# Second graph-attention layer: 2048 of its destinations through a dense edge matrix, edge weights kept in one place

## What is computed

```
h = x @ W                                   # 6250 x 64
logits = leaky_relu(al_s[src] + al_d[dst], 0.2)
alpha = exp(logits - max) / sum(exp(logits - max))     # per destination, self-loops included
out = segment_sum(h[src] * alpha, dst) + b
x = layernorm(x + (out @ Wf + bf))
```

## Time and profile before

| | us |
|---|---|
| median of 3 runs | 7316.36 |
| lowest, highest | 7312.23, 7317.64 |
| profiled execution, its span (no other time is given for it) | 7334.6 |
| PE, DVE, ACT, POOL busy in it | 6062.9, 3365.6, 1425.8, 5086.1 |

### The profile page before, as it was taken

The page is one execution under the profiler, slowest core; times in us unless marked ns, Lnnn a source line. Parts: engine busy times, 40 slices in busy tenths (PEclk is TensorE's granted clock), DMA queues, the critical chain, the costliest instruction groups (busy, mean ns, idle before and its releaser), DMA issues. The chain is left out here.

```text
span 7334.6 us, 120792 instructions
## 1 busy us (share of the span) xinstructions
PE 6062.9 (83%) x30188; PEld 4280.8 (58%) x30188; DVE 3365.6 (46%) x13118; ACT 1425.8 (19%) x5109; POOL 5086.1 (69%) x4839
## 2 busy tenths in 40 slices
PE   3888888886728888867877779998899999988997
PEld 2555555555615555556666656665566656665665
DVE  4444444443436666645555544444233323333444
ACT  2333333332201222212222211111000100010001
POOL 3777777777737777757777757665777677767776
PEclk9887888887869999965555569998999999999998
DMA  8988899884324444433333359885999799979996
GB/s 290 217 186 187 183 191 188 185 184 109 93 83 114 117 116 116 116 77 81 82 81 80 83 159 303 284 282 177 308 311 308 240 316 307 303 240 318 312 318 216
DMA packets 767060, 1440.91 MB, mean 196 GB/s; under 512 B 157272, under 2 KB 484876, under 8 KB 764212
## 3 DMA queue, kind: packets, MB, share of 16 engines
q1 hardware_dynamic: 474532, 886.97, 35.9%
q0 software_dynamic: 289936, 523.75, 32.0%
q10 hardware_dynamic: 2304, 26.74, 0.9%
HBM read 1140.97 MB, written 295.98 MB: 196 GB/s over the span
## 5 line engine op out<-in xcount | busy, mean ns | idle before, releaser
L736 POOL DMA_INDIRECT rows<-gcn_rows,index x1632 | 1550.7, 950 | 664.1 <-issue 457.4
L1277 POOL DMA_INDIRECT rows<-gat_rows,index x1568 | 1500.6, 957 | 646.1 <-issue 459.4
L832 PEld LDWEIGHTS bank<-onehots,rows 128*128 128x128 f32 x8704 | 1146.5, 194 | 598.0 <-issue 539.2
L1608 POOL DMA_INDIRECT support<-rows,index x784 | 1218.7, 1554 | 388.0 <-DMA support<-rows,index 188.2
L832 PE MATMUL bank<-onehots,rows 128*128 128x128 f32 x8704 | 1185.4, 279 | 150.0 <-DVE onehots L881 66.5
L1408 PE MATMUL bank<-onehots,rows 128*128 128x128 f32 (+1 forms) x4704 | 949.6, 339 | 325.3 <-DVE rows L1484 325.1
L1408 PEld LDWEIGHTS bank<-onehots,rows 128*128 128x128 f32 (+1 forms) x4704 | 722.7, 203 | 527.2 <-issue 322.2
L844 PE MATMUL dense_bank<-matrix,edge_space 128*128 128x512 f32 x1792 | 891.2, 619 | 0.0
L1747 PE MATMUL rows_bank<-x_window,cross 128*128 128x256 f32 x1568 | 649.8, 506 | 94.9 <-ACT cross L1725 94.2
L736 POOL DMA_INDIRECT rows<-norm,index x544 | 517.0, 950 | 283.2 <-issue 152.9
L844 PE MATMUL dense_bank<-alpha,edge_space 128*128 128x512 f32 x1344 | 671.4, 621 | 13.5 <-DVE acc L899 13.5
(11 more groups left out here) (306 smaller groups left out, 7408.1 us busy)
## 6 DMA issues: line engine op xcount, KB each, us to landing
matrix<-matrix SPq DMA_DIRECT2D x448, 512.0 KB, 3.9
alpha<-matrix SPq DMA_DIRECT2D x336, 512.0 KB, 4.3
matrix<-zeros SPq DMA_DIRECT2D x196, 512.0 KB
edge_space<-gcn_rows SPq DMA_DIRECT2D x588, 128.0 KB
dst_row<-in_dst_flat SPq DMA_DIRECT2D x100, 512.0 KB
source_row<-in_src_flat SPq DMA_DIRECT2D x198, 256.0 KB, 5.3
support<-zeros ACTq DMA_DIRECT2D x16, 1632.0 KB, 28.0
rows<-gcn_rows,index POOLq DMA_INDIRECT x1632, 5.2
```

What stands on the lines that cost most here:

```text
L736: nc.gpsimd.indirect_dma_start(rows[:, k, :], None, table, bass.IndirectOffsetOnAxis(ap=index[:, k:k + 1], axis=0),).then_inc(gathered[k], 16)
L832: done = nc.tensor.matmul(by_chunk(banks[h])[:, c, :], rows[:, k, c * P:(c + 1) * P], onehots[:, k, :], start=first and c == 0, stop=final ...
L1277: nc.gpsimd.indirect_dma_start(rows[:, k, :], None, table, bass.IndirectOffsetOnAxis(ap=index[:, k:k + 1], axis=0),).then_inc(gathered[k], 16)
L1608: nc.gpsimd.indirect_dma_start(support[k % COPIES], bass.IndirectOffsetOnAxis(ap=index[:, k // HALF, k % HALF:k % HALF + 1], axis=0), rows ...
```

## The change

- The second attention layer gets its own function, `dense_attention_pass`, unrolled, with the 34 turns of the dense passes and 196 steps. The edge's weight depends on the source, the destination and how many equal edges there are, so a step needs only the matrix's **count**: with the source's share taken into the table once (`scaled_table`), the weight of a pair is count x (1 + relu(ratio_dst x ratio_src - 1)), times a factor of the destination applied per group of 512.
- A step therefore loads 512 KB (four slots), VectorE shifts the count out of the gate word (`count`), ScalarE makes the relu term (`above_one`), VectorE joins both (`share`), and TensorE makes one matmul 65x512 (`step`). Before the first turn TensorE, VectorE and ScalarE prepare `ratio` and `source_ratio`. At the end POOL clears the borrowed half of `g.acc`.
- The edge's weight is kept only in the rows' 65th column: one exponential for a batch instead of two, and the scaling reads it from there. The index copies are gone; POOL's gathers read `g.source`.
- `pe_third` comes after tile 5 of a half, and `dve_late` and `dve_later` come directly behind each other at the end of a half. Two blocks can be worked on in a turn. Four blocks are left for after the last turn, besides the one under way.
- The gate word now holds gate/4 with the count in its top two bits. In `degrees`, VectorE packs it, and POOL's writes wait for that (`s.packed`). A flag `windows_after` repeats passes if a pair has more than three equal edges.
- The three gate passes therefore mask the word before use: `strip`, one 128x512 VectorE operation for each step into four contiguous slots, and TensorE reads those. The group's sum is multiplied by 4 when it is added. The semaphore `group_summed` is folded into `steps_used`.
- Many signatures get both a running number `j` and a block `b`.

```diff
+                    if packed:
+                        pe.wait_ge(s.strip_ready, q + 1)
+                    values = stripped[q % STRIPPED] if packed else values_of(n, value)
                     for c in range(2):
-                        done = nc.tensor.matmul(dense_banks[c][:, 0:GROUP], table_rows[:, n, c * P:(c + 1) * P],
-                                                matrix[n].rearrange("p (n v) -> p n v", v=2)[:, :, value],
+                        done = nc.tensor.matmul(dense_banks[c][:, 0:GROUP], table_rows[:, n, c * P:(c + 1) * P], values,
                                                 start=row == 0, stop=row == steps_of_group - 1)
-                    if row == steps_of_group - 1:
-                        done.then_inc(s.group_summed, 1)
-                    else:
-                        done.then_inc(s.steps_used, 1)
+                    done.then_inc(s.steps_used, 1)
...
+                            for q in strips_after.get((i * RING + k) // BATCH, []) if packed else []:
+                                strip(q)
+                def strip(q):
+                    dve.wait_ge(step_loaded[q % SLOTS], 32 * (q // SLOTS + 1))
+                    if q >= STRIPPED:
+                        dve.wait_ge(s.steps_used, q - STRIPPED + 1)
+                    nc.vector.tensor_scalar(stripped[q % STRIPPED].bitcast(INT32), values_of(q % SLOTS, 1).bitcast(INT32),
+                                            2 ** COUNT_BIT - 1, None, ALU.bitwise_and).then_inc(s.strip_ready, 1)
...
+                        if packed:
+                            done = nc.vector.scalar_tensor_tensor(here, sums, SHRINK, here, ALU.mult, ALU.add)
+                        else:
+                            done = nc.vector.tensor_tensor(here, here, sums, ALU.add)
...
+def dense_attention_pass(nc, g, table, **fields):
...
+            def _(pool):
+                for t in range(loops):
+                    for k in range(RING):
+                        if k % BATCH == 0:
+                            pool.wait_ge(s.summed, t * batches + (k // BATCH + 1))
+                            pool.sem_inc(s.issued, 1)
+                        at = t * RING + k
+                        nc.gpsimd.indirect_dma_start(
+                            rows[:, k, :], None, table,
+                            bass.IndirectOffsetOnAxis(ap=g.source[:, at:at + 1], axis=0),
+                        ).then_inc(gathered[k], 16)
+                pool.wait_ge(s.group_added, GROUPS)
+                nc.gpsimd.memset(aside, 0.0)
...
+                def load_step(q):
+                    if q >= slots:
+                        sync.wait_ge(s.counted, q - slots + 1)
+                    sync.dma_start(matrix[q % slots], by_step[:, q, :]).then_inc(step_loaded[q % slots], 16)
...
+                def exponentials(u):
+                    batch = u % batches
+                    act.wait_ge(s.exponent_ready, u + 1)
+                    nc.scalar.activation(rows[:, batch * BATCH:(batch + 1) * BATCH, features:features + 1],
+                                         exponent[:, batch, :, :], ACT.Exp).then_inc(s.weight_ready, 1)
+                def above_one(q):
+                    group, row = divmod(q, g.rows)
+                    low = low_of(group) - low_block * P
+                    if q >= 2:
+                        act.wait_ge(s.share_ready, q - 1)
+                    nc.scalar.activation(above[:, q % 2, :], ratio[:, low:low + GROUP], ACT.Relu,
+                                         bias=minus_one[:], scale=source_ratio[:, row:row + 1]
+                                         ).then_inc(s.above_ready, 1)
...
+                for u in range(loops * batches):
+                    half, second = divmod(u, per_half)
+                    b, late = started.get(half), finished.get(half)
...
+                    if b is not None and not second:
+                        ends.act_own(act, s, number[b], b)
+                    for q in steps_of.get(u, []):
+                        above_one(q)
+                    exponentials(u)
+                    if late is not None and not second:
+                        ends.act_left(act, s, number[late], late)
+                    if b is not None and second:
+                        ends.act_clear(act, s, number[b], b, zeros)
+                    if late is not None and second:
+                        ends.act_late(act, s, number[late], late)
+                        ends.act_later(act, s, number[late], late)
...
+                def step(q):
+                    group, row = divmod(q, g.rows)
+                    if q == 0:
+                        pe.wait_ge(s.table_ready, 1)
+                    if row == 0 and group:
+                        pe.wait_ge(s.group_added, group)
+                    pe.wait_ge(s.share_ready, q + 1)
+                    nc.tensor.matmul(dense_bank, scaled_table[:, row, :], shares[:, q % 3, :], start=row == 0,
+                                     stop=row == g.rows - 1).then_inc(s.steps_used, 1)
...
+                    for k in range(RING):
+                        half, at = 2 * t + k // HALF, k % HALF
+                        b, late = started.get(half), finished.get(half)
+                        multiply(t, k)
+                        if at == BATCH - 1:
+                            shares_of(half + 1)
+                        if b is not None and at == 3:
+                            if group_of(b):
+                                pe.wait_ge(s.group_added, group_of(b))
+                            ends.pe_first(pe, s, number[b], b, 2 * t + 1 + k // HALF)
+                        if late is not None and at == 5:
+                            ends.pe_third(pe, s, number[late], late)
+                        if b is not None and at == 7:
+                            ends.pe_second(pe, s, number[b], b)
+                        if k % BATCH == BATCH - 1:
+                            for q in steps_of.get(t * batches + k // BATCH, []):
+                                step(q)
...
+                def count(q):
+                    dve.wait_ge(step_loaded[q % slots], 16 * (q // slots + 1))
+                    if q >= 2:
+                        dve.wait_ge(s.share_ready, q - 1)
+                    word = matrix[q % slots].rearrange("p (n v) -> p n v", v=2)[:, :, 1]
+                    nc.vector.tensor_scalar(counts[q % 2], word.bitcast(INT32), COUNT_BIT, None, ALU.logical_shift_right
+                                            ).then_inc(s.counted, 1)
+                def share(q):
+                    dve.wait_ge(s.above_ready, q + 1)
+                    dve.wait_ge(s.counted, q + 1)
+                    if q >= 3:
+                        dve.wait_ge(s.steps_used, q - 2)
+                    nc.vector.scalar_tensor_tensor(shares[:, q % 3, :], above[:, q % 2, :], 1.0, counts[q % 2],
+                                                   ALU.add, ALU.mult).then_inc(s.share_ready, 1)
...
+                def batch_of(u):
+                    t, batch = divmod(u, batches)
+                    these = steps_of.get(u, [])
+                    slice_of = slice(batch * BATCH, (batch + 1) * BATCH)
+                    for q in these[:1]:
+                        count(q)
+                    for k in range(slice_of.start, slice_of.stop):
+                        dve.wait_ge(gathered[k], t * 16 + 16)
+                    dve.wait_ge(s.shared, 2 * t + (batch // per_half + 1))
...
+                    nc.vector.tensor_tensor(other, d, top, ALU.add)
+                    nc.vector.tensor_tensor(to, rows[:, slice_of, features:features + 1], d, ALU.add
+                                            ).then_inc(s.own, 1)
+                    for q in these[1:]:
+                        count(q)
+                    dve.wait_ge(s.own, 2 * u + 1)
+                    nc.vector.scalar_tensor_tensor(other, other, 0.2, other, ALU.mult, ALU.max)
+                    nc.vector.scalar_tensor_tensor(to, to, 0.2, to, ALU.mult, ALU.max).then_inc(s.own, 1)
+                    for q in these[:1]:
+                        share(q)
+                    dve.wait_ge(s.own, 2 * u + 2)
+                    nc.vector.tensor_tensor(to, to, other, ALU.subtract).then_inc(s.exponent_ready, 1)
+                    dve.wait_ge(s.summed, u + 1)
+                    for k in range(slice_of.start, slice_of.stop):
+                        tile = t * RING + k
+                        made = nc.vector.tensor_scalar(onehots[:, k, :], g.iota[:], g.half_offset[:, tile:tile + 1],
+                                                       None, ALU.is_equal)
+                    made.then_inc(s.onehot_ready, 1)
+                    dve.wait_ge(s.weight_ready, u + 1)
+                    here = rows[:, slice_of, 0:features]
+                    nc.vector.tensor_tensor(here, here, rows[:, slice_of, features:features + 1]
+                                            .to_broadcast([P, BATCH, features]), ALU.mult).then_inc(s.scaled, 1)
```

(64 more changed lines are left out.)

534 lines of the change are left out of this document (370 added, 164 removed).

## The result

| | kernel before | changed kernel |
|---|---|---|
| median of four runs, us | 7317.0 (7312.2 to 7318.1) | 7410.4 (7394.4 to 7413.6) |
| ratio, 95% interval | | 1.0126 (1.0111 to 1.0140) |
| span of the profiled execution, us | 7334.6 | 7409.5 |

The change makes the kernel 1.3% slower, clear of the interval. I had forecast 7199 and a range up to 7310: wrong in sign and in range.

A forecast was written before the change was run, and what follows sets the result against it. VectorE was to become the second attention layer's bound: 738 us of work plus 162 of stalls made turns of 900, the layer 967 against 1100.6. With -134 + 2 + 15 = -117, 7316 became 7199 us, range 7060 to 7310.

The forecast's parts named there:

- Stalls of VectorE, (a): Second attention layer's turns: `dve_late` waits for `pe_third`, which comes two tiles later; 2.0 x 44 = 88 us.
- (b): Second layer's turns: `dve_later` no longer covered by a batch, ScalarE reloads its exponential table behind it; 1.0 x 44 = 44 us.
- (c): Second layer's turns: late destination rows, TensorE held at each group's start, SyncE's queue; together 30 us (0 to 70).
- VectorE's work: Second layer's turns: measured pieces sum to 738 us without stalls, 21.7 a turn, over POOL's 19.8, so VectorE becomes the bound.
- TensorE's clock: Second layer's turns: TensorE needs 29.2 us a turn at the half clock, half of that at the full, mostly full assumed.
- The rival with TensorE at the half clock as the bound: Second layer: turns 1003 us, layer 1070 (-31), kernel 7302; chance 0.14.
- All my rivals for the layer: Second layer: few stalls, kernel 7074 (chance 0.15); TensorE bound at the half clock, kernel 7302 (chance 0.14).
- strips that hold up POOL in the gate passes: Gate passes: at 0.3 us lost for a strip, +176, kernel 7360, slower than before; chance 0.12.
- passes repeated by the flag: Gate passes: if the new flag were raised, four passes would be repeated, over 2000 us; chance 0.01.
- Head and tail: Second layer's ends: first batch at some 11.6 us, and 55.3 us from the last scaling to the next pass.
- Packing: Before POOL's first write: it now waits for four dependent operations of 245 elements; +2 us.
- The gate passes: Three gate passes: faster contiguous matmul records against gathers slowed by strips; +5 us a pass, +15 (bounds -48 and +288).

The follow-up runs named there:

- the other three moves: Changed kernel with third stage ahead of share records and steps, own row loaded early, first stage ahead of the shares: layer 884.6 us against 1170.7.
- four edits: Changed kernel with third stage and first stage moved ahead of shares, own row and exponential table loaded early: layer 862.5 us; kernel 7096.2 against 7320.4 before, ratio 0.9699.

## Why the prediction was wrong

- **Stalls of VectorE, (a): the step that failed.** I wrote that `pe_third` comes "only after two more tiles", and priced tiles, four records and the handing over: 2.0 us, 88 in all. Measured in the turns: 4.4 us a wait, 188 in 43 waits (206 with the blocks behind the turns). In TensorE's queue there also stand, since VectorE last released it, sixteen share records and one or two steps: 3.4 and 1.9 us in the half shown. I had both durations, in the sum for TensorE's work, and did not set them ahead of the third stage. The move of that stage alone, -104, takes the changed kernel from slower than before to slightly faster. It does not bring the 7199 that I forecast; for that the next item is needed too.
- **(b) and (c).** The table I put at 44; loading it early gave 22, on top of the other three moves. "SyncE's queue" with two other items I put at 30. The own row, moved behind a wait for shares, was worth 101 by itself. VectorE's waits for the clearing (76 us) had no term at all. The sum of the stalls was 162 with a top of 290; three waits alone measure 360 in the same stretch.
- **VectorE's work** was right, and slightly too high: `share` 687 ns (0.69 forecast), `count` 431 to 435 (0.49 forecast), its busy time in the layer 679 us, less than my 738, which counts from start to start and leaves the ends out. That it would be the bound does not follow from this: no engine was.
- **TensorE's clock.** "I take mostly the full clock" failed too: 0.68, though well above the 0.54 of before. A TensorE that waits for VectorE in each half idled 132 us of 500 in the stretch from 3500, and its work ran on at mixed levels. The rival with TensorE at the half clock as the bound gave 1003 us of turns; they took 1098, so it wasn't that either. All my rivals for the layer had a single full engine, where the real one had none, and none of them had it slower than before. The 0.15 that I gave to a slower kernel lay with strips that hold up POOL in the gate passes, with passes repeated by the flag, and with what I did not see; the gate passes are only 13 us longer.
- **Head and tail:** 13.2 us to the first batch (11.6 forecast), 59.7 from the last scaling to the next pass (55.3). Small terms, both low. With the 1098 between them they make the layer's 1171.
- **Packing** (+2): not to be seen beside the scatter of 24 us in where the layer starts.
- **The gate passes** (+15): measured +13.1, with both effects. Records 0.430 apart instead of 0.450 as forecast, 16 us a pass of TensorE's time. Gathers 42 ns longer, 23 us a pass, where I had taken 20. The strips take 0.42 us each, 247 us for 588 of them, and the gathers lost 69. By the Trainium skill ("SBUF — State Buffer", Who interferes with whom) an operation of this kind can hold the port pair that it shares with POOL for its whole length, if it is first to take it, and POOL then stands still. With POOL held through every strip, an estimate by that rule, it would be the whole 247. The trace agrees in kind, at 28% of this bound.

## What to carry to other kernels

Before pricing a new wait, write down for each engine, in its own order, everything that stands between the event that releases it and the instruction that the other side needs, and do the same for the DMA queue. A sum of busy times gives a floor, and a layer whose engines hand over to each other several times in each half may lie far above it: here the turns took 1098 us against 738 of VectorE's own work, with no engine full. Then the order of instructions can be worth more than their number: four edits, which remove no work, took 308 us of 1171, where a cut of 137 us of VectorE's work took 11. A move can also cost while another obstacle stands and gain once it is gone, so moves have to be tried in combination.

## What the runs showed of the hardware

- Less work for TensorE made the layer slower. With its step records an eighth as wide, the granted clock went from 0.78 to 0.53, each tile record from 306 to 413 ns, and the layer from 862.5 to 911.8 us. TensorE's busy time in the layer rose from 700 to 707 us, with 182 us less of step records. On the changed kernel the same edit took the clock from 0.68 to 0.52 and still gained 39 us; there a step stood ahead of the third stage, for which VectorE waited. The Trainium skill ("TensorE: Matmul & The Clock Gate", Part 1) says that the low rate is the default and activity lifts it; both pairs fit that, less matmul work going with a lower granted clock.
- A 512-wide one-input integer operation of VectorE costs POOL time even where its gathers take only 74% of the stretch: with 588 of them the gathers took 69 us more, 0.12 us each.
- A 512-wide fp32 matmul record took 0.430 us with contiguous operands and 0.450 where it read every second word, in the gate passes with and without strips, at a granted clock near 1.
